# Two column groups summed side by side, adjacency work put ahead of the layer norm's moments, and the first rounding on VectorE in two parts

## The reference

```python
def _layernorm(x, axis=-1, eps=1e-05):
    m = jnp.mean(x, axis=axis, keepdims=True)
    v = jnp.var(x, axis=axis, keepdims=True)
    return (x - m) / jnp.sqrt(v + eps)

h = jnp.maximum(_layernorm(x, axis=-1), 0.0)      # x is 4096 x 256, fp32
agg = jnp.matmul(adj, h)                          # adj is 4096 x 4096, fp32
out = x + relu(jnp.matmul(agg, W.T) + b)          # W is 256 x 256
```

## Time and profile before

| what | us |
|---|---|
| median of 3 runs (380.98 to 381.16) | 381.09 |
| the profiled execution | 380.8 |
| its span, first to last instruction | 379.0 |
| PE busy | 375.1 |
| DVE busy | 212.2 |
| ACT busy | 181.8 |
| POOL busy | 50.1 |

### The profile page before, as it was taken

One profiled execution on the slowest core, in us unless ns is written; L12 is line 12 of the kernel. 1 busy time (PEld: TensorE's weight loads), 2 busy tenths in 40 slices (PEclk: granted clock), 3 DMA queues, 4 the chain that ended last, 5 costly groups with the idle time before them and its releaser, 6 DMA issues.

```text
span 379.0 us, 4516 instructions
## 1 busy us (share of the span) xinstructions
PE 375.1 (99%) x1651; PEld 308.1 (81%) x1651; DVE 212.2 (56%) x294; ACT 181.8 (48%) x228; POOL 50.1 (13%) x88
## 2 busy tenths in 40 slices
PE   8999999999999999999999999999999999999997
PEld 4888888888888888888888888888888888888885
DVE  5999988874744453535564544444464444444424
ACT  5888776764443434343643343433355243434341
POOL 5687732320010000000001000000000100000000
PEclk9999999999999999999999999999999999999999
DMA  7989877577659565655566856565656775555203
GB/s 263 369 301 304 275 256 258 185 235 256 210 186 317 174 215 178 208 177 209 176 206 207 294 178 209 178 205 184 201 189 195 256 242 195 187 202 185 92 2 111
DMA packets 22774, 80.25 MB, mean 212 GB/s; under 512 B 2496, under 2 KB 2880, under 8 KB 22752
## 3 DMA queue, kind: packets, MB, share of 16 engines
q1 hardware_dynamic: 19584, 68.30, 54.1%
q0 software_dynamic: 3168, 11.67, 8.6%
HBM read 75.76 MB, written 4.19 MB: 211 GB/s over the span
## 4 chain that ended last, share of the span: by engine, by line
PE 98%; DMA 1%; DVE 0%; ACT 0%; POOL 0%; issue 0%; POOLq 0%
PE bank L421 92%; PE bank L463 6%; DMA x_sb<-x_dram 1%; ACT adj_hi L346 0%; POOL rstd L204 0%; ACT h_sb L352 0%; DVE out_sb L320 0%; DVE stats L240 0%; DVE mean_var L245 0%; DVE var_eps L249 0%; POOLq L200 0%
## 5 line engine op out<-in xcount | busy, mean ns | idle before, releaser
L421 PE MATMUL bank<-adj_hi,h_sb 128*128 128x512 f32 x1024 | 254.3, 389 | 0.2 <-ACT adj_hi L346 0.2
L229 DVE TENSOR_TENSOR adj_lo<-adj_in,adj_hi 128x1024 fp32r<-128x1024 f32 x126 | 154.6, 1227 | 145.7 <-ACT adj_hi L342 145.5
L421 PEld LDWEIGHTS bank<-adj_hi,h_sb 128*128 128x128 f32 x1024 | 192.0, 188 | 40.5 <-issue 0.5
L342 ACT ACTIVATE adj_hi<-adj_in 128x1024 fp32r<-128x1024 f32 x126 | 133.5, 1060 | 176.7 <-PE bank L421 174.5
L421 PE MATMUL bank<-adj_lo,h_sb 128*128 128x512 f32 x512 | 137.5, 389 | 0.0
L421 PEld LDWEIGHTS bank<-adj_lo,h_sb 128*128 128x128 f32 x512 | 96.1, 188 | 20.0
L204 POOL TENSOR_TENSOR rstd<-var_eps,minus_half 128x1 f32<-128x1 f32 x32 | 30.5, 954 | 3.4 <-DVE var_eps L249 0.8
L221 POOL DMA_DIRECT2D out_t_dram<-out_sb x3 | 2.2, 726 | 211.0 <-DVE out_sb L320 211.0
L352 ACT ACTIVATE h_sb<-centred,rstd 128x256 fp32r<-128x256 f32 x32 | 16.0, 499 | 3.6 <-POOL rstd L204 3.2
L362 ACT ACTIVATE centred<-x_sb,neg_mean 128x256 f32<-128x256 f32 x31 | 15.5, 500 | 2.1 <-DVE neg_mean L264 1.9
L270 DVE SCALAR_TENSOR_TENSOR h_sb<-centred,rstd,h_sb 128x256 fp32r<-128x256 f32 x32 | 15.3, 477 | 1.0 <-ACT h_sb L352 1.0
(11 more groups left out here) (25 smaller groups left out, 42.7 us busy)
## 6 DMA issues: line engine op xcount, KB each, us to landing
adj_in<-adj_t_dram SPq DMA_DIRECT2D x126, 512.0 KB, 3.6
xt_sb<-x_t_dram POOLq DMA_DIRECT2D x4, 1024.0 KB, 7.4
x_sb<-x_dram POOLq DMA_DIRECT2D x7, 512.0 KB, 6.5
out_t_dram<-out_sb POOLq DMA_DIRECT2D x3, 1024.0 KB, 4.9
adj_in<-adj_t_dram SPq DMA_DIRECT2D x4, 256.0 KB, 4.8
out_t_dram<-out_sb SPq DMA_DIRECT2D x3, 256.0 KB, 2.0
x_sb<-x_dram POOLq DMA_DIRECT2D x3, 128.0 KB, 4.6
w_sb<-w_t_dram POOLq DMA_DIRECT2D x1, 256.0 KB, 6.0
```

Source lines behind the costliest of these rows:

```text
L229: nc.vector.tensor_tensor(adj_lo[:, k, :], adj_in[:, k, :], adj_hi[:, k, :].bitcast(fp32), ALU.subtract).then_inc(s_lo, 1)
L342: nc.scalar.activation(adj_hi[:, k, :], adj_in[:, k, :], ACT.Copy).then_inc(s_hi, 1)
L421: last = nc.tensor.matmul(bank(g, kb, c)[:], h_sb[:, t, hp, kb * P:(kb + 1) * P], adj_parts[ap][:, n % U, chunk(c)], start=(t == 0 and (hp ...
```

## The change

The steps are now entries of a table, `UNITS`. For tiles 0 to 23 the steps of groups 0 and 1 alternate (unit 2t is group 0 tile t, unit 2t+1 is group 1 tile t); then come tiles 24 to 31 of group 0, then those of group 1, then groups 2 and 3 as before. The splits and outputs follow four and eight units behind the end of each group.

The lists of VectorE and ScalarE for the 32 tiles are reordered. VectorE's loop for n = 2 to 32 is `adj_rest(n)`, `h_rest(n-1)`, moments and minus mean of n. ScalarE's is `adj_rounded(n)`, `centre(n-1)`, `h_rounded(n-1)`. GpSimd's computing is the same; it issues the loads of x for tiles 2 to 7 after its first power, not before it.

VectorE rounds the first adjacency chunk in two parts of 256 columns, and TensorE's first pass takes them one by one with matmuls of 256 columns. The warm-up matmuls behind the first landing are two, not three. The five semaphores of the last stores become one.

```diff
-    WARM_ON = 3
+    WARM_ON = 2
...
+    UNITS = [(g, t) for t in range(TILES - LAG) for g in range(2)]
+    UNITS += [(g, t) for g in range(2) for t in range(TILES - LAG, TILES)]
+    UNITS += [(g, t) for g in range(2, GROUPS) for t in range(TILES)]
...
         def _(pool):
-            for i in range(1, U):
-                load_x(pool, i)
+            load_x(pool, 1)
...
                 root(t)
                 if t == 0:
-                    load_x(pool, U)
+                    for i in range(2, U + 1):
+                        load_x(pool, i)
...
+            def first_rounded():
+
+                dve.wait_ge(s_early[0][0], 16)
+                nc.vector.tensor_copy(adj_hi[:, 0, 0:HALF], adj_in[:, 0, 0:HALF]).then_inc(s_quarter, 1)
+                nc.vector.tensor_copy(adj_hi[:, 0, HALF:BANK], adj_in[:, 0, HALF:BANK]).then_inc(s_hi, 1)
...
             centre_first()
+            first_rounded()
             h_rest(0)
+            early_rest(0, 0)
+            early_rest(0, 1)
             moments(1)
             minus_mean(1)
-            early_rest(0, 0)
-            early_rest(0, 1)
-            moments(2)
-            minus_mean(2)
-            h_rest(1)
             early_rest(1, 0)
             early_rest(1, 1)
-            moments(3)
-            minus_mean(3)
-            adj_rest(2)
-            h_rest(2)
-            for t in range(3, TILES):
-                if t + 1 < TILES:
-                    moments(t + 1)
-                    minus_mean(t + 1)
-                adj_rest(t)
-                h_rest(t)
+
+            for n in range(EARLY, TILES + 1):
+                adj_rest(n)
+                h_rest(n - 1)
+                if n < TILES:
+                    moments(n)
+                    minus_mean(n)
...
             h_rounded(0)
-            early_rounded(0, 0)
+
+            act.wait_ge(s_hi, 1)
             early_rounded(0, 1)
+            early_rounded(1, 0)
             centre(1)
-            early_rounded(1, 0)
-            h_rounded(1)
             early_rounded(1, 1)
-            for t in range(EARLY, TILES):
-                centre(t)
-                adj_rounded(t)
-                h_rounded(t)
+            for n in range(EARLY, TILES + 1):
+                adj_rounded(n)
+                if n > EARLY:
+                    centre(n - 1)
+                h_rounded(n - 1)
```

More of the change, by code:

```diff
@@ L29, in bass_preln_gnn_residual @@
     BANK = 512
+    HALF = BANK // 2
     CHUNKS = 2
@@ L37, in bass_preln_gnn_residual @@
     WARM_UP = 10
-    WARM_ON = 3
+    WARM_ON = 2
     EARLY = 2
+    LAG = 8
     SPLIT_AT = 4
     OUT_AT = 8
+    UNITS = [(g, t) for t in range(TILES - LAG) for g in range(2)]
+    UNITS += [(g, t) for g in range(2) for t in range(TILES - LAG, TILES)]
+    UNITS += [(g, t) for g in range(2, GROUPS) for t in range(TILES)]
     X_PIECES = [(t, t + 1) for t in range(4)] + [(t, t + 4) for t in range(4, TILES, 4)]
@@ L103, in bass_preln_gnn_residual @@
         s_hlo = sem("h_lo_made")
+        s_quarter = sem("first_adj_quarter_made")
         s_hi = sem("adj_hi_made")
@@ L114, in bass_preln_gnn_residual @@
         s_out = sem("out_stored")
-        s_last = [sem(f"out_stored_last{i}") for i in range(SUMS + 1)]
+        s_last = sem("last_group_stored")
         block = ctx.enter_context(nc.Block())
@@ L128, in x_piece, with end_of, made_chunk, made_unit @@
             return next(i for i, (a, b) in enumerate(X_PIECES) if a <= t < b)
-        def made_chunk(t, c):
-            return CHUNKS * t + c + 1
-        def made_tile(n):
+        def end_of(g):
+            return max(n for n, u in enumerate(UNITS) if u[0] == g) + 1
+        SPLIT = {end_of(g) + SPLIT_AT: g for g in range(LAST)}
+        OUT = {end_of(g) + OUT_AT: g for g in range(LAST)}
+        def made_chunk(n, c):
+            return CHUNKS * n + c + 1
+        def made_unit(n):
             return made_chunk(n, CHUNKS - 1) if n < EARLY else CHUNKS * EARLY + n - EARLY + 1
@@ L157, in _, with load_chunk @@
         def _(sp):
-            def load_chunk(t, c):
-                sp.dma_start(adj_in[:, t, chunk(c)], adj_v[:, t, chunk(c)]).then_inc(s_early[t][c], 16)
+            def load_chunk(n, c):
+                g, t = UNITS[n]
+                at = g * GW + c * BANK
+                sp.dma_start(adj_in[:, n, chunk(c)], adj_v[:, t, at:at + BANK]).then_inc(s_early[n][c], 16)
             def load_adj(n):
-                g, t = divmod(n, TILES)
+                g, t = UNITS[n]
                 if n >= U:
-                    sp.wait_ge(s_hi, made_tile(n - U))
-                    sp.wait_ge(s_lo, made_tile(n - U))
+                    sp.wait_ge(s_hi, made_unit(n - U))
+                    sp.wait_ge(s_lo, made_unit(n - U))
                 sp.dma_start(adj_in[:, n % U, :], adj_v[:, t, g * GW:(g + 1) * GW]).then_inc(s_adj[n % U], 16)
@@ L173, in _ @@
             load_chunk(1, 1)
-            for n in range(EARLY, GROUPS * TILES):
+            for n in range(EARLY, len(UNITS)):
                 load_adj(n)
@@ L180, in _ @@
                 at = LAST * GW + c * BANK
-                sp.dma_start(out_v[:, o, at + a:at + b], out_sb[:, o, within(c, a, b)]).then_inc(s_last[i], 16)
-            for s in s_last:
-                sp.wait_ge(s, 16)
+                sp.dma_start(out_v[:, o, at + a:at + b], out_sb[:, o, within(c, a, b)]).then_inc(s_last, 16)
+            sp.wait_ge(s_last, 16 * len(pieces(LAST)))
         @block.gpsimd
         def _(pool):
-            for i in range(1, U):
-                load_x(pool, i)
+            load_x(pool, 1)
             nc.gpsimd.memset(minus_half[:], -0.5).then_inc(s_const, 1)
@@ L227, in adj_rest, with early_rest @@
                 k = n % U
-                dve.wait_ge(s_hi, made_tile(n))
+                dve.wait_ge(s_hi, made_unit(n))
                 nc.vector.tensor_tensor(adj_lo[:, k, :], adj_in[:, k, :], adj_hi[:, k, :].bitcast(fp32),
                                         ALU.subtract).then_inc(s_lo, 1)
[L232 to L235, removed]
+            def first_rounded():
+                dve.wait_ge(s_early[0][0], 16)
+                nc.vector.tensor_copy(adj_hi[:, 0, 0:HALF], adj_in[:, 0, 0:HALF]).then_inc(s_quarter, 1)
+                nc.vector.tensor_copy(adj_hi[:, 0, HALF:BANK], adj_in[:, 0, HALF:BANK]).then_inc(s_hi, 1)
+            def early_rest(n, c):
+                dve.wait_ge(s_hi, made_chunk(n, c))
+                nc.vector.tensor_tensor(adj_lo[:, n, chunk(c)], adj_in[:, n, chunk(c)],
+                                        adj_hi[:, n, chunk(c)].bitcast(fp32), ALU.subtract).then_inc(s_lo, 1)
             def moments(t):
@@ L322, in make_out @@
                                                    op0=ALU.max, op1=ALU.add).then_inc(s_sum, 1)
[L324 to L330, removed]
+            for n in range(TILES + 1, len(UNITS)):
+                if n in SPLIT:
+                    sums_rest(SPLIT[n])
+                if n in OUT:
+                    make_out(OUT[n])
+                adj_rest(n)
             sums_rest(LAST)
@@ L342, in adj_rounded, with early_rounded @@
                 nc.scalar.activation(adj_hi[:, k, :], adj_in[:, k, :], ACT.Copy).then_inc(s_hi, 1)
-            def early_rounded(t, c):
-                act.wait_ge(s_early[t][c], 16)
-                nc.scalar.activation(adj_hi[:, t, chunk(c)], adj_in[:, t, chunk(c)], ACT.Copy).then_inc(s_hi, 1)
+            def early_rounded(n, c):
+                act.wait_ge(s_early[n][c], 16)
+                nc.scalar.activation(adj_hi[:, n, chunk(c)], adj_in[:, n, chunk(c)], ACT.Copy).then_inc(s_hi, 1)
             def h_rounded(t):
@@ L385, in sums_rounded @@
                 if g < LAST:
-                    act.wait_ge(s_pe, (g + 1) * TILES)
+                    act.wait_ge(s_pe, end_of(g))
                 for i, (c, kb) in enumerate(GROUP_BANKS):
@@ L400, in _ @@
             act.wait_ge(s_b, 16)
[L401 to L407, removed]
+            for n in range(TILES + 1, len(UNITS)):
+                if n in SPLIT:
+                    sums_rounded(SPLIT[n])
+                if n in OUT:
+                    add_bias(OUT[n])
+                adj_rounded(n)
             add_bias(LAST)
@@ L415, in _, with add_up @@
             adj_parts = (adj_hi, adj_lo)
-            def add_up(g, t, chunks, hp, ap):
-                n = g * TILES + t
+            def add_up(n, chunks, hp, ap):
+                g, t = UNITS[n]
                 for kb in range(KB):
@@ L425, in add_up, with first_sums, early_unit, sum_unit @@
                 return last
[L427 to L442, removed]
+            def first_sums(cols):
+                for kb in range(KB):
+                    nc.tensor.matmul(bank(0, kb, 0)[:, cols], h_sb[:, 0, 0, kb * P:(kb + 1) * P],
+                                     adj_hi[:, 0, cols], start=(cols.start == 0), stop=False,
+                                     skip_group_check=True)
+            def early_unit(n):
+                pe.wait_ge(s_hhi, 1)
+                if n == 0:
```

(41 more changed lines are left out.)

## The result

The changed kernel takes 399.63 us (median; 399.41 to 400.57) against 381.03 for the kernel before, timed beside it: 1.0491 times as long, 95% interval 1.048 to 1.0501, or 18.6 us more. The forecast was 400.2. The profiled execution took 399.65, its span is 397.9; the spans differ by 18.9 us.

What follows compares the result with a forecast made beforehand. TensorE's unbroken chain from 5.84 us bounded the kernel; the new circle makes it wait for VectorE. 380.8 + 18.0 (circle) + 1.1 (W) = 399.9, plus 0.3 for the median: 400.2 us; range 395 to 405, a little over 8 in 10.

Steps and rivals of the forecast that it cites:

- The circle: Tile loop: adjacency rest, power, ScalarE's h, rest of h, moments wait in a ring; 3.36 us against TensorE's 2.72, loss 18.0.
- The rival without a hold: Tile loop: power not held by the adjacency rest, round 2.51 us, TensorE never waits; 380.8 us, chance 0.10.
- the one with alternating rounds: Tile loop: power starts first in every other round, rounds 2.30 and 3.66, mean 2.98 us; 389.2 us, chance 0.04.
- that sign: Tile loop: forecast wrong if rests stand 2.72 us apart or powers of 0.55 us are among those before unit 32.
- The hold: Tile loop: VectorE's adjacency rest, started 0.24 us ahead, blocks GpSimd's power, which then takes 1.40 us, not 0.55.
- Where it starts: Early tile loop: adjacency rest 3 starts between 12.6 and 13.15 us; 13.15 taken as start of 29 rounds.
- W: Splitting of W: unit 33 needs an adjacency rounding behind W's rounding on ScalarE; TensorE loses 1.1 us.
- The start: First chunk's 256-column VectorE cast, 0.3 us: first real matmul at 5.5, not 5.84; between 0 and 0.45 us remains.
- The second chunk: Start: its rounding begins when it lands, 6.04 before, ending 6.67; a gate on the first chunk's lead.
- The rest of h: Start: VectorE's rest of h(0), at 5.10 before, now waits behind both casts; a second gate on the lead.
- The alternation: Alternating groups 0 and 1 costs TensorE nothing; outputs 8 units apart, 21.8 us, cover VectorE's 8 rests of 9.8 us.

Runs made afterwards that it cites:

- e5: Changed kernel; from step 3 VectorE waits for GpSimd's epsilon add, then makes three one-column instructions before each adjacency rest; 380.55 us, ratio to before 0.9991.
- e1: Changed kernel with VectorE's moments one tile further ahead (step n makes those of n+1); 380.74 us, ratio to before 0.9995.
- e4: e1 with the old start: ScalarE rounds the first chunk whole, matmuls of 512, three warm-up matmuls; 380.77 us, ratio to before 0.9994.
- e7: Changed kernel with h made a tile later, h of tile 1 ahead of adjacency 2, unit 2's h-rest pass first; 380.63 us, ratio to before 0.999.
- e6: Kernel before with only the unit order changed (groups 0 and 1 alternate, outputs following each group's end); 380.96 us, ratio 1.0004.
- e2: Changed kernel; from step 3 VectorE waits for GpSimd's epsilon add and writes one column before each adjacency rest; 405.17 us, ratio to before 1.064.

## Why the prediction was right, point by point

**The circle.** Predicted 3.36 us a round. Measured from rest 3 at 12.47 to rest 32 at 110.50: 98.0 us over 29 rounds, 3.38; 28 of them lie between 3.36 and 3.39. Each piece stands in the round shown above: power's end at 1.64, h 0.51, rest of h to next adjacency rest 1.15. The rival without a hold is what e5 comes to with a wait added; the one with alternating rounds didn't occur. The 26 waits of TensorE that the profile names between 14 and 110 us all end with adjacency rests, as said.

**One round of 3.62**, at 42.85, I had not foreseen. Timeline of the changed kernel:

```profile
42.83 1.28 POOL L216 TENSOR_TENSOR var_eps<-mean_var,eps_sb 128x1 f32<-128x1 f32 x1 [1.18 <-DVE mean_var L270]
42.85 1.22 DVE L248 TENSOR_TENSOR adj_lo<-adj_in,adj_hi 128x1024 fp32r<-128x1024 f32 x1
...
44.19 0.56 POOL L222 TENSOR_TENSOR rstd<-var_eps,minus_half 128x1 f32<-128x1 f32 x1
```

The rest held the epsilon add, and the power ran free behind it; 0.25 us more than holding the power alone. The prediction said that it would be wrong if a power of 0.55 us stood before unit 32, and that 1.40 would hold throughout. Taken by the letter that sign came, once: 0.56 us at 44.19. The hold was there too, but on the instruction before. The sign should have been a round under 2.72.

**Where it starts.** I took rest 3 at 13.15 and bounded it by 12.6. It started at 12.47, outside that bound: the piece of step 2 landed at 8.82, ScalarE began on it at once behind its own list, and rest 2 started at 10.19, not 10.85. In e1 and e4 the same piece landed at 9.86 and 9.89, so landings here move by a microsecond between runs of like starts; a bound of half a microsecond was too narrow. This error (-0.7) and the longer rounds (+0.6) cancel almost. That the total came within 0.3 us of the sum for the profiled execution (399.65, predicted 399.9) is therefore partly luck. The 0.3 that the forecast added for the median was not there: the median is 399.63. Unit 32's adj-lo matmul came at 111.80 (predicted 112.0), 17.8 us later than in the earlier trace rows.

**W.** Predicted 1.1. Measured: unit 33 was taken up at 115.48, where 111.80 + 2.72 = 114.52 would have been due: 1.0. As said, it waited for an adjacency rounding behind W's rounding:

```profile
112.60 0.62 ACT L400 ACTIVATE w_hi<-w_sb 128x512 fp32r<-128x512 f32 x1
...
114.22 1.19 PE L440 MATMUL bank<-adj_hi,h_sb 128*128 128x512 f32 x4 [0.28 <-ACT adj_hi L361]
```

**The start.** The cast of 256 columns takes 0.29 us (taken: 0.3):

```profile
4.90 0.29 DVE L254 CAST adj_hi<-adj_in 128x256 fp32r<-128x256 f32 x1 [0.94 <-DMA adj_in<-adj_t_dram]
```

The first real matmul starts at 5.34 (predicted 5.5; the chunk landed 0.17 us earlier), 0.50 ahead of before, and step 2 starts at 11.34 against 11.45: 0.11 is left of it, within the 0 to 0.45. The second chunk took most of it, as predicted. Timeline of the changed kernel:

```profile
6.67 0.19 PEld L440 LDWEIGHTS bank<-adj_hi,h_sb 128*128 128x128 f32 x1 [0.52 <-ACT adj_hi L365]
```

The matmul ahead of the second chunk starts at 6.19, 0.43 us ahead of its place before (6.61). The first of the second chunk starts at 6.67 and before at 6.85, 0.18 ahead; two matmuls on 0.07 is left. The rest of h held nothing: its pass starts at 5.89, 0.12 behind the last matmul of 256 columns. In e1 it was step 2's h, and in e7 the clock, that took a lead. For the result none of it counted, as said, since TensorE later waited for VectorE anyway.

**The alternation** and the outputs eight units apart: predicted covered. e6 shows it for the lists before, and e1 for the changed ones.

## What to carry to other kernels

When a pipeline runs over several engines, look in each engine's list for the distance between an instruction and the one that needs its far result: if one round of the loop closes a circle of waits, its latency, not any engine's busy time, sets the pace (here VectorE was 69% busy and TensorE waited for it). A tiny instruction on GpSimd beside a long two-input one on VectorE should be priced, if it starts second, as ending some 0.4 us behind the end of the long one (1.24 + 0.40 here); putting it first, by a wait or by order, can be worth far more than the wait. And a hold costs only where something waits for the held instruction. The kernel before and e1 had long powers too, 2.3 us a round, and VectorE got ahead through them and then had short ones, because each rest waited for ScalarE. In the changed kernel the hold stood in the circle, so VectorE never got ahead and never left the long powers.

## What the runs showed of the hardware that was not expected

- A held power ends where the rest decides, not where it began. With a the start of the rest of 1024 columns, it ended at a + 1.63 when both started level (e5 at 49.98), at a + 1.65 when it started 0.04 later (e2 at 59.07), at a + 1.63 when it started 0.20 later (e2 at 62.80, 1.43 long) and at a + 1.64 when it started 0.24 later (the changed kernel at 50.07).
- The hold went one way only: rests that started 0.15 to 0.20 us behind a power took 1.22 and 1.23 us (e5 at 20.72, the kernel before at 53.62), as long as rests alone.
- The margin by which the order is decided is small: a power 0.15 us ahead of the rest was free (e5), one level with it or 0.04 us behind was held for 1.6 us (e5, e2). For the epsilon add, 0.03 us ahead was enough in the usual round (53.17 against 53.20), while 0.02 us ahead was held for 1.28 us (42.83 against 42.85). That is at the limit of what the profile's starts can tell.
- With the same ten warm-up matmuls, TensorE's step from 1.2 to 2.4 GHz came before the first real matmuls in some profiled runs and among them in others. Read from the distances of matmuls of 256 columns: 0.11 us already on constants in the kernel before and the changed one; 0.21 on constants in e7 and e5, and still 0.21 on the first real ones.
